# Attention scores and maxima from float32 queries and keys in four strips of 32 rows

## What is computed

```python
q = _rope((x @ Wq.T).reshape(B, S, H, hd).transpose(0, 2, 1, 3))   # 16 heads of 16
k = _rope(...)
scores = jnp.einsum('bhqd,bhkd->bhqk', q, k) * scale
scores = jnp.where(causal, scores, jnp.finfo(scores.dtype).min)
attn = jax.nn.softmax(scores, axis=-1)
out = jnp.einsum('bhqk,bhkd->bhqd', attn, v)
```

## Time and profile before

| | us |
|---|---|
| median of 3 runs | 3296.63 (3295.2 to 3301.05) |
| the profiled execution | 3297.0, span 3295.2 |
| TensorE busy | 3071.7 (93%) |
| VectorE busy | 2252.1 (68%) |
| ScalarE busy | 1763.6 (54%) |
| GpSimd busy | 329.8 (10%) |

### The profile page before, as it was taken

One profiled execution on the slowest core, in us unless ns is written; L12 is line 12 of the kernel. 1 busy time (PEld: TensorE's weight loads), 2 busy tenths in 40 slices (PEclk: granted clock), 3 DMA queues, 4 the chain that ended last, 5 costly groups with the idle time before them and its releaser, 6 DMA issues.

```text
span 3295.2 us, 45435 instructions
## 1 busy us (share of the span) xinstructions
PE 3071.7 (93%) x17679; PEld 1544.8 (47%) x17679; DVE 2252.1 (68%) x4403; ACT 1763.6 (54%) x3199; POOL 329.8 (10%) x193
## 2 busy tenths in 40 slices
PE   5799999999889999998989999999997999999899
PEld 2433334447553333453854333344575433334468
DVE  4788887562678888756368888856546888885632
ACT  2366666564236666645514666654540566665560
POOL 3200000210400000111130000012122000002200
PEclk9799999999999999999999999999999999999999
DMA  4322201015502220002542202000443220100052
GB/s 129 99 40 40 40 2 39 14 52 197 149 20 40 40 40 27 20 7 95 190 119 46 39 9 40 27 20 7 151 163 103 40 41 11 31 27 27 9 179 81
DMA packets 123555, 201.89 MB, mean 61 GB/s; under 512 B 10094, under 2 KB 106996, under 8 KB 120232
## 3 DMA queue, kind: packets, MB, share of 16 engines
q1 hardware_dynamic: 110820, 148.58, 13.9%
q10 hardware_dynamic: 12520, 50.40, 8.2%
HBM read 156.01 MB, written 42.16 MB: 60 GB/s over the span
## 4 chain that ended last, share of the span: by engine, by line
PE 74%; DVE 17%; ACT 4%; issue 2%; POOL 1%; DMA 1%; ACTq 0%; SPq 0%; DVEq 0%; POOLq 0%
PE ps L694 14%; DVE pm L1269 12%; PE ps L674 10%; PE ps L614 9%; PE ps L795 7%; PE ps L850 7%; PE ps L627 6%; PE ps L881 3%; PE ps L870 3%; PE ps L574 2%; PE ps L738 2%; PE ps L659 2%; PE ps L678 1%; PE ps L808 1%; PE ps L603 1%
## 5 line engine op out<-in xcount | busy, mean ns | idle before, releaser
L1269 DVE TENSOR_REDUCE pm<-ps 128x1 f32<-128x512 f32 (+4 forms) x2560 | 1376.9, 602 | 273.6 <-PE ps L614 181.9
L983 ACT ACTIVATE R<-ps 128x512 f32<-128x512 f32 (+1 forms) x2240 | 1175.5, 593 | 603.0 <-PE ps L674 412.1
L674 PE MATMUL ps<-R 99*128 99x512 bf16 (+3 forms) x2560 | 827.9, 349 | 10.7 <-ACT R L983 6.0
L614 PE MATMUL ps<-R 96*128 96x512 bf16 x1536 | 578.6, 387 | 46.2 <-DVE pm L1269 40.7
L694 PE MATMUL ps<-R 128*17 128x512 f32 (+3 forms) x5120 | 528.9, 531 | 0.0
L614 PEld LDWEIGHTS ps<-R 96*128 96x128 bf16 x1536 | 147.3, 97 | 446.4 <-DVE pm L1269 372.0
L674 PEld LDWEIGHTS ps<-R 99*128 99x128 bf16 x2560 | 241.4, 97 | 146.0 <-ACT R L983 64.1
L694 PEld LDWEIGHTS ps<-R 128*17 128x17 f32 x5120 | 117.8, 96 | 280.1 <-issue 168.3
L850 PE MATMUL ps<-R 128*128 128x512 f32 x512 | 231.7, 610 | 14.0 <-ACT R L1050 13.9
L627 PE MATMUL ps<-R 128*128 128x257 f32 x1024 | 237.4, 388 | 4.1 <-ACT R L934 3.6
L795 PE MATMUL ps<-snT,R 128*128 128x512 f32 x512 | 230.1, 593 | 0.0
(11 more groups left out here) (151 smaller groups left out, 3321.7 us busy)
## 6 DMA issues: line engine op xcount, KB each, us to landing
R<-in_L_ffn_w_dram SPq DMA_DIRECT2D x64, 1024.0 KB, 5.8
R<-q_parts ACTq DMA_DIRECT2D x12, 768.0 KB
R<-k_parts ACTq DMA_DIRECT2D x12, 768.0 KB
R<-in_L_attn_x_dram SPq DMA_DIRECT2D x16, 512.0 KB, 8.4
q_parts<-R SPq DMA_DIRECT2D x16, 512.0 KB, 3.6
k_parts<-R SPq DMA_DIRECT2D x16, 512.0 KB, 3.4
R<-in_L_attn_x_dram SPq DMA_DIRECT2D x4, 2048.0 KB, 8.3
x_park<-R SPq DMA_DIRECT2D x16, 512.0 KB, 2.6
```

What stands on the lines that cost most here:

```text
L614: last = mm(ps[:, bank, :], qt(4 * c + r), kt(4 * kc, 4), start=True, stop=True)
L674: last = mm(bank[:, i * w:(i + 1) * w], kst[g % 2][0:BROWS, h0 + i, j * P:(j + 1) * P], qst[g % 2][0:BROWS, h0 + i, (c + 1) * CH - w:(c + ...
L983: A(Eb[s % ESLOTS][:, h0:h0 + n, 0:w], ps[:, u % NST, 0:n * w].rearrange("p (n w) -> p n w", n=n), ACT.Exp, scale=SCALE).then_inc(s_ex, 1)
L1269: mx = lambda o, i: V.tensor_reduce(o, i, AX.X, ALU.max)
```

## The change

Queries and keys stay float32. They are parked and loaded as 16 rows per head, and each head of a group has its own 32 partitions (16 rows of the head, one more for ones or the negated maximum), so that four heads lie in four strips of rows of the array. All four groups have their own place in SBUF. The three parts go, with the casts, remainders, thirds and the splitting of the maximum. Scores and maxima are float32 products with 17 and 16 rows. A mask product would need 128 rows; it is cut into four strips of 32 rows (`strips` holds the identity, `maskq` and `maskk` the mask), each product with a strip for the rows of its own head, on as many columns as that part of the mask touches; scores are masked in pairs of heads (`mask_units`). "odd" and "even" become "near" (512 columns) and "edge" (256), each reduced at once, and the four heads follow one another inside each kind, in the order 2, 3, 0, 1. The last two diagonal steps of a chunk become one of 384 columns; every unit is one head. There are 144 steps of four units instead of 160, 576 units instead of 560, and 592 maxima as before; `WEIGHED` holds the pairs of steps, with the last step alone. The core of the diff:

```diff
-    return 4 * (k % NC) + 4
-
-
-STEPS = [(k, j) for k in range(NK) for j in range(steps_of_chunk(k))]
+    c = k % NC
+    return [(j,) for j in range(4 * c + 2)] + [(4 * c + 2, 4 * c + 3)]
+
+
+STEPS = [(k, js) for k in range(NK) for js in steps_of_chunk(k)]
...
-    for h in range(HG):
-        yield k, h, "diag", 0, 0
-        yield k, h, "odd", 0, 0
-        yield k, h, "even", 0, 0
-        for kc in range(c):
-            for r in range(4):
-                yield k, h, "full", r, kc
-
-
+    blocks = [("diag", 0, 0), ("near", 0, 0), ("edge", 0, 0)]
+    blocks += [("full", r, kc) for kc in range(c) for r in range(4)]
+    for kind, r, kc in blocks:
+        for h in (2, 3, 0, 1):
+            yield k, h, kind, r, kc
...
-    behind = 8
+    behind = 10
...
-WEIGH_BEHIND, EVAC_BEHIND, TURN_BEHIND, GATHER_BEHIND = 3, 5, 8, 9
+WEIGH_BEHIND, EVAC_BEHIND, TURN_BEHIND, GATHER_BEHIND = 4, 5, 8, 9
...
-        kst = [view(R1, 8192 * i, 4096, bf16).rearrange("p (h t) -> p h t", h=HG) for i in range(2)]
-        qst = [view(R1, 8192 * i + 4096, 4096, bf16).rearrange("p (h t) -> p h t", h=HG) for i in range(2)]
+        kg = [view(R1, 4096 * g, 2048) for g in range(NG)]
+        qg = [view(R1, 4096 * g + 2048, 2048) for g in range(NG)]
...
-            heads = slice(HG * g, HG * g + HG)
-            for a, n, at in ((0, 48, 0), (48, 16, 0), (64, 32, 0)):
-                eng.dma_start(qst[g % 2][a:a + n, :, tokens], q_park[at:at + n, heads, tokens]).then_inc(loaded, 16)
-            for a, n, at in ((0, 48, 0), (48, 32, 16), (80, 16, 32), (96, 3, 48)):
-                eng.dma_start(kst[g % 2][a:a + n, :, tokens], k_park[at:at + n, heads, tokens]).then_inc(loaded, 16)
+            for h in range(HG):
+                rows = slice(32 * h, 32 * h + HD)
+                eng.dma_start(kg[g][rows, tokens], k_park[:, HG * g + h, tokens]).then_inc(loaded, 16)
+                eng.dma_start(qg[g][rows, tokens], q_park[:, HG * g + h, tokens]).then_inc(loaded, 16)
+            eng.dma_start(kg[g][HD:P:32, tokens], ones_park[:, tokens]).then_inc(loaded, 16)
+
+        GROUP_LOADS = 16 * (2 * HG + 1)
...
-            sp.dma_start(pmask, mask_in).then_inc(s_w2, 16)
-            sp.dma_start(pmaskT, maskT_in).then_inc(s_w2, 16)
+            for h in range(HG):
+                for dst, src in ((pstrips, ident_in), (pmaskq, mask_in[:, 0:P]), (pmaskk, maskT_in)):
+                    sp.dma_start(dst[32 * h:32 * h + 32, :, :], src.rearrange("(a r) c -> r a c", r=32)).then_inc(s_w2, 16)
...
-                        park = (q_park, k_park)[qk][0:PROWS].rearrange("(x i) h t -> (i h) x t", i=HD // 2)
-                        first, third = ((0, 4), (2, 0))[qk]
-                        sp.wait_ge(s_p1, b * QU + i + 1)
-                        sp.dma_start(park[:, first:first + 4, tokens], rope_parts[set_of(b, i)]).then_inc(s_pk[set_of(b, i)], 16)
-                        sp.wait_ge(s_p2[qk], b * NC + c + 1)
-                        sp.dma_start(park[:, third:third + 2, tokens],
-                                     rope_rest[set_of(b, i)].rearrange("p (x t) -> p x t", t=CH)).then_inc(s_pk[set_of(b, i)], 16)
+                        park = (q_park, k_park)[qk].rearrange("(f i) h t -> (i h) f t", f=2)
+                        sp.wait_ge(s_rr, b * QU + i + 1)
+                        sp.dma_start(park[:, :, tokens], rope_prod[set_of(b, i)][:, 0:2, :]).then_inc(s_pk[set_of(b, i)], 16)
...
-                    return qst[g % 2][0:KROWS, h, i * P:(i + 1) * P]
+                    return qg[g][32 * h:32 * h + KROWS, i * P:(i + 1) * P]
 
                 def kt(i, n):
-                    return kst[g % 2][0:KROWS, h, i * P:(i + n) * P]
+                    return kg[g][32 * h:32 * h + KROWS, i * P:(i + n) * P]
                 if kind == "rows":
                     pe.wait_ge(s_nm, b * NK + (k + 1))
-                    last = tr(ps[0:PARTS * HG * 4, bank, 0:P // 2].bitcast(bf16),
-                              negp[:, :, :, :].rearrange("p h s t -> p (h s t)"), identb[:, :])
+                    last = tr(ps[0:HG * 4, bank, 0:P], negm[:, :, :].rearrange("p h t -> p (h t)"), ident[:, :])
                 elif kind == "diag":
-                    mm(ps[:, bank, :], identb[:, :], maskb[:, :, :].rearrange("p r t -> p (r t)"),
-                       start=True, stop=True)
+                    rows = slice(32 * h, 32 * h + 32)
+                    for a in range(4):
+                        mm(ps[:, bank, :].rearrange("p (r t) -> p r t", t=P)[:, :, 32 * a:P], strips[rows, a, :],
+                           maskq[rows, a:a + 1, 32 * a:P].to_broadcast([32, 4, P - 32 * a]),
+                           start=a == 0, stop=True, skip_group_check=True)
                     for i in range(4):
                         last = mm(ps[:, bank, i * P:(i + 1) * P], qt(4 * c + i), kt(4 * c + i, 1),
                                   start=False, stop=True, skip_group_check=True)
-                elif kind == "odd":
+                elif kind == "near":
+                    mm(ps[:, bank, 0:2 * P], qt(4 * c + 2), kt(4 * c, 2), start=True, stop=True)
+                    last = mm(ps[:, bank, 2 * P:4 * P], qt(4 * c + 3), kt(4 * c, 2), start=True, stop=True)
+                elif kind == "edge":
                     mm(ps[:, bank, 0:P], qt(4 * c + 1), kt(4 * c, 1), start=True, stop=True)
-                    last = mm(ps[:, bank, P:4 * P], qt(4 * c + 3), kt(4 * c, 3), start=True, stop=True)
-                elif kind == "even":
-                    last = mm(ps[:, bank, 0:2 * P], qt(4 * c + 2), kt(4 * c, 2), start=True, stop=True)
+                    last = mm(ps[:, bank, P:2 * P], qt(4 * c + 3), kt(4 * c + 2, 1), start=True, stop=True)
                 else:
...
-                    s, h0, n, w = UNITS[u]
-                    k, j = STEPS[s]
+                    s, h = UNITS[u]
+                    k, js = STEPS[s]
                     g, c = divmod(k, NC)
-                    if s == FIRST_STEP[k] and u == FIRST_UNIT[s]:
-                        pe.wait_ge(s_bias[k % 3], (b * BIAS_USES[k % 3] + k // 3 + 1) * 64)
+                    if s == FIRST_STEP[k] and h == 0:
+                        pe.wait_ge(s_bias[k % 2], (b * BIAS_USES[k % 2] + k // 2 + 1) * 64)
                     if u >= NST:
                         pe.wait_ge(s_ex, b * SU + (u + 1 - NST))
-                    bank = ps[:, u % NST, :]
-                    for i in range(n):
-                        last = mm(bank[:, i * w:(i + 1) * w], kst[g % 2][0:BROWS, h0 + i, j * P:(j + 1) * P],
-                                  qst[g % 2][0:BROWS, h0 + i, (c + 1) * CH - w:(c + 1) * CH],
-                                  start=i == 0, stop=True, skip_group_check=True)
-                    if diagonal(s) >= 0:
-                        last = mm(bank[:, 0:n * w].rearrange("p (n w) -> p n w", n=n)[:, :, 0:P], identb[:, :],
-                                  maskTb[:, 0:n, :], start=False, stop=True, skip_group_check=True)
-                    last.then_inc(s_st, 1)
+                    rows = slice(32 * h, 32 * h + BROWS)
+                    for j, at, w in tiles_of_step(s):
+                        last = mm(ps[:, u % NST, at:at + w], kg[g][rows, j * P:(j + 1) * P],
+                                  qg[g][rows, (c + 1) * CH - w:(c + 1) * CH], start=at == 0, stop=True, skip_group_check=True)
+                    if not diagonal(s):
+                        last.then_inc(s_st, 1)
+                    elif h % 2:
+                        mask_units(u - 1, u)
+
+                def mask_units(*pair):
+
+                    for a in range(4):
+                        for u in pair:
+                            s, h = UNITS[u]
+                            rows = slice(32 * h, 32 * h + 32)
+                            n = len(tiles_of_step(s))
+                            bank = ps[:, u % NST, :].rearrange("p (n w) -> p n w", n=2)
+                            last = mm(bank[:, 0:n, 0:32 * a + 32], strips[rows, a, :],
+                                      maskk[rows, a:a + 1, 0:32 * a + 32].to_broadcast([32, n, 32 * a + 32]),
+                                      start=False, stop=True, skip_group_check=True)
+                            if a == 3:
+                                last.then_inc(s_st, 1)
 
                 def weigh(s):
 
-                    k, j = STEPS[s]
+                    k, js = STEPS[s]
                     g, c = divmod(k, NC)
-                    w = CH - max(diagonal(s), 0) * P
-                    if j == 0:
+                    if s == FIRST_STEP[k]:
                         if k:
                             pe.wait_ge(s_ev, b * NK + k)
                         else:
                             pe.wait_ge(s_vone, b + 1)
                     pe.wait_ge(s_ex, b * SU + (LAST_UNIT[s] + 1))
...
-                for u, (s, h0, n, w) in enumerate(UNITS):
-                    if u == FIRST_UNIT[s] and s >= ESLOTS:
+                for u, (s, h) in enumerate(UNITS):
```

(41 more changed lines are left out.)

167 lines of the change are left out of this document (63 added, 104 removed).

## The result

The changed kernel takes 5659.52 us (median of 4 runs, 5643.62 to 5666.81) against 3298.23 beside it: a ratio of 1.7153, interval 1.7112 to 1.7194. The direction was as forecast. The size was not: 3650 us were forecast, with 4250 as the upper end, and the change costs 2361 us and not 354.

A forecast was written before the change was run, and what follows sets the result against it. Loop bound by a coupling: first block's latency, VectorE's reductions, last score, weighting alone. 168 + 66 + 40 + 62 + 48 - 32 - 14 + 16 = +354 on 3297.0 gave 3650 us; range 3430 to 4250.

The forecast's parts named there:

- The full clock: Attention loops: granted clock taken as 1.00 from the earlier trace; anything below would upset every term; no size or chance given.
- Strips run side by side: Scores and maxima: four heads' float32 halves run together, 0.22 us per call's share; the rival without concurrency, 5800 us, had 5%.
- two wide: Rival for scores and maxima: float32 calls start 0.43 us apart, 4240 us; 14% together with its in-between cases.
- The long cycle: Loop cycles of eight scores and maxima plus weighting: 7.00 us, some 0.75 longer in 224 cycles, +168 us.
- Short cycles: Last diagonal steps, four units instead of three: +1.1 us in each of 60 cycles, +66 us.
- Masks of the maxima and scores: Mask strips at diagonal blocks: +40 us for maxima, 0 for scores; upper end for uncovered score pairs +270.
- Last chunk: Scores without maxima: cycles from 5.20 to 6.5 us, +42, and transposes and projections between, +20; +62 us in all.
- 72 x 0.3: Last chunk: transposes and projections using all array rows wait for what is in flight, +20 us.
- Early maxima and prologue: Maxima between combination tiles and values: +48 us; prologue: -14 for the masks' cast, +16 for early maxima at low clock.
- the latency is hidden: Rival in the cycles: VectorE finds blocks ready as soon as now, TensorE's column time decides; 3187 us, 12%.
- The checks it named: Signs: starts in fours, VectorE waiting about a microsecond, cycles of 7.0 us, VectorE below 65%, last chunk near 72 us.

The follow-up runs named there:

- e3: The changed kernel with scores and maxima contracting over all 32 rows of their strip instead of 17 and 16, plus a memset at the start: 4492.41 us.
- e9: The kernel of e3 without any mask matmul, of maxima or scores: 4158.14 us.
- e10: The changed kernel with 32 rows per strip, heads of the maxima exchanged within each four, and no mask matmuls: 4053.87 us.
- e6: The kernel of e3 with the heads exchanged within each four maxima, so a maximum is meant to lie two strips from the next score: 4335.87 us.
- e8: The kernel of e2 with all 32 rows of a strip in use: 3766.13 us.
- e2: The changed kernel with scores and maxima reading only the upper bfloat16 half of each float32 query and key, one instruction per call: 3902.42 us.
- e15: The kernel before with scores contracting over the last 35 of their 99 rows and maxima over the last 32 of their 96: 4624.16 us.
- e11: The kernel of e3 with the maxima's mask as one matmul over the whole array, the scores' masks still in strips: 4752.05 us.

## Why the prediction was wrong

**The full clock: failed, and most of the error.** The prediction took the granted clock of the earlier trace rows over into the changed kernel and said itself that anything below would upset every term. It named no rival for it and gave it no chance. Nothing in the trace of before showed products with few rows beside a clock, since there were none in number; the low clock in the earlier trace rows stands where TensorE does nothing. The runs put 1168 us of the 2010 that were missed on it (after less e3), and part of it still remains in e3, with 764 us at 1.2 GHz against 127 before.

**Strips run side by side: right.** Even in the changed kernel, products of 512 columns start in fours some 240 times. In e9 it shows without the masks between. e9, one cycle at a clock of 1.00:

```profile
263.51 1.91 PE L696 MATMUL ps<-R 128*17 128x512 f32 x16
265.35 0.69 PE L606 MATMUL ps<-R 32*128 32x512 f32 x1
265.36 0.69 PE L666 MATMUL ps<-R 32*128 32x512 f32 x1
265.36 0.69 PE L606 MATMUL ps<-R 32*128 32x512 f32 x1
265.37 0.69 PE L666 MATMUL ps<-R 32*128 32x512 f32 x1
265.88 0.59 PE L606 MATMUL ps<-R 32*128 32x512 f32 x1
...
271.11 1.91 PE L696 MATMUL ps<-R 128*17 128x512 f32 x16
```

VectorE in the same cycle:

```profile
266.51 5.09 DVE L1234 TENSOR_REDUCE pm<-ps 128x1 f32<-128x512 f32 x8 [3.15 <-PE ps L606]
```

Four first halves start within 0.02 us, the second ones 0.52 later (0.43 forecast). So neither "two wide" nor the Trainium skill's rule of a strict order of starts ("TensorE: Matmul & The Clock Gate", Part 3) holds: by that rule a fourth call's first half could not start before the first call's second, if the halves stand in the program call by call, as the kernel writes its calls; the trace itself doesn't show the program's order.

**The long cycle: right in kind, too short in two places.** The first block is ready 1.16 us after its start (1.07 forecast), eight reductions take 5.09 (4.80), and the cycle is 7.60; the usual one of this sort in e10 is 7.3 (7.00 forecast). That is 0.3 us in each of 224 cycles, some 67 us. But cycles with "near", "edge" and "diag" are longer than the model of full maxima, which the forecast used for all: over the 196 long cycles of e10 that lie wholly at the full clock the mean is 7.73, against 6.24 before. The step is 1.49 us where 0.75 was forecast, 0.74 x 224 = 166 us in all.

**Short cycles: size wrong.** +1.1 us was forecast. Before they have a mean of 3.27 us, in e10 at the full clock 5.66: +2.4, or 1.3 x 56 = 73 us more than the term.

**Masks of the maxima and scores: size wrong.** The forecast had 0.78 us for a diagonal maximum, at VectorE's pace with three banks, and +40 in all, with +310 at both upper ends. The chain of twelve instructions in one head's rows sets the pace instead: 1.07 us. All masks together cost 334 us beside no mask at all. The kernel before has masks too (262144 columns, an estimated 110 us at 0.42 ns each), so that over it the strips cost 224 to 334 us: near the upper end or above it, and not the 40 of the sum.

**Heads that meet in the same rows: not in the forecast.** It assumed that neighbours in TensorE's order always have different heads. There are 592 maxima and 576 units, so the two sequences slide past each other. It cost 104 to 157 us at nearly the full clock (e10, e6).

**Last chunk: size wrong.** From a batch's last full maximum to its last score it is 55.9 us before; the forecast adds 15.5, which makes 71. e10 has 88 to 100, a mean of 93, at mean clocks of 0.79 to 0.92. The four chunks have the lower level for 102 us, which explains 51 of the missing 86 us at most. For the rest the step is "72 x 0.3": e10's shortest cycles there, those without other work between, take 6.2 us (6.7 by the forecast's terms), but between products over all rows a score stands alone, and then its whole latency counts. e9's last chunk:

```profile
763.48 1.12 PE L666 MATMUL ps<-R 32*128 32x512 f32 x2
764.53 1.99 PE L740 MATMUL ps<-wogT,R 128*128 128x256 f32 x8
766.46 1.13 PE L666 MATMUL ps<-R 32*128 32x512 f32 x4
```

One score holds the array for 1.05 us (763.48 to 764.53), 0.83 more than a bfloat16 one's 0.22. Against the 0.3 of the sum that is an estimated 72 x 0.53 = 38 us.

**Early maxima and prologue: right.** From a batch's last score to the next batch's first (or the end) e3 takes 53 us more than the kernel before, all four together, and its first score comes 15 us later, of which some 17 are its memset. The terms gave 50.

**A sum in a rival: wrong.** The rival "the latency is hidden" took 55 us off for fewer columns in "near" and "edge". There are as many as in "odd" and "even", 196608. The terms that are left give -41 in place of -96, and the rival 3242 us instead of 3187. The forecast did not use that term.

**The checks it named.** Starts in fours, a wait of about a microsecond (in e9; at the lower clock it is two) and VectorE's share below 65% came true (39%); cycles of 7.0 and a last chunk near 72 did not. Of the rivals none describes what happened.

**What stays open.** From after to e10 the causes measured are 1168 (rows), 334 (masks) and 104 (heads), in this order: 5660 - 1606 = 4054. Against the forecast without its mask term (3610) 444 us remain, and more if the masks that the kernel before still has are taken off it. Cut at each batch's first score, last full maximum and last score, e10 takes 569 us more than the kernel before in the loops (202 forecast), 148 in the last chunks (62 forecast) and 40 elsewhere (50 forecast). So the rest lies in the loops, 367 us, and in the last chunks, 86. In the loops longer cycles (166) and short ones (73) are measured, and the 191 us at the lower clock there explain at most half of themselves, 96; some 30 are not assigned. Why the clock of e8 stays at 0.812 is open too. e3, and e8 beside e2, show that rows in use move this kernel's clock; how the chip weighs them, what else it counts, and whether it is the number of rows or what stands in them, was not tried.

## What to carry to other kernels

Before packing small products into strips, ask how many rows of the array they will keep in use: here 17 rows at a time, with TensorE 98% busy, had the clock at half for 62% of the time, and work that had nothing to do with the strips paid for it too (the weighting, 531 to 875 ns). Keep strip products and whole-array products apart, since a change between them costs the latency of what is in flight (1.05 us for a lone score, e9); and when parts of a change are not tied to its main idea, measure them alone: here two of them made the kernel before 0.56% faster.

## What the runs showed that was not expected

- The granted clock falls with few rows in use while TensorE is 98% busy: 0.60 in the loop with 16 and 17 rows per strip, 0.90 with 32 (e3), by the same instructions. The added rows of e3 hold zeros or leftovers, so it isn't useful work that counts. In the kernel before it is 1.00 with 96 and 99 rows and 0.59 with 32 and 35 (e15), where the changes between two row counts are a second difference.
- Between bfloat16 calls of 512 columns with 32 and with 35 rows it is 0.32 us at 2.4 GHz and 0.54 at 1.2 GHz; between two with 32 rows 0.22 and 0.40 (e15), and between 96 and 99 rows 0.22 (before).
- Halves of float32 products in different strips of rows overtake one another: four first halves within 0.02 us, the second ones 0.52 later (e9).
- One mask product over all rows between strip products costs 0.85 us more than four in strips (1.92 against 1.07 us per diagonal maximum, e11 and e3).
